# One even state of eight handled like the odd ones in a selective-scan recurrence

## The reference, cut to what matters

```python
delta = softplus(dt @ w_dt)
deltaA = exp(delta[..., None] * A)                       # decay, one per state n of 16
deltaBu = delta[..., None] * B[:, :, None, :] * u[..., None]   # input, "drive"
def step(h, ab):
    a, bu = ab
    h = a * h + bu
    return (h, h)
...                                                      # scan over the 128 steps of a sequence
y = einsum('bldn,bln->bld', hs, C) + u * D               # states weighed by C, summed over n
return y * silu(res) @ w_out
```

## Time and profile before

| what | value |
|---|---|
| median of three runs | 2059.17 us |
| the profiled execution's own time | 2061.6 us |
| its span | 2059.8 us |
| PE busy | 1955.6 us (95%) |
| VectorE busy | 1422.5 us (69%) |
| GpSimd busy | 1208.6 us (59%) |
| ScalarE busy | 929.9 us (45%) |
| first scan starts, last close starts | 1352.1 us, 1744.40 us |
| scans on VectorE | 128 of 1224 ns and 128 of 1196 ns |

### The profile page before, as it was taken

One profiled execution on the slowest core, in us unless ns is written; L12 is line 12 of the kernel. 1 busy time (PEld: TensorE's weight loads), 2 busy tenths in 40 slices (PEclk: granted clock), 3 DMA queues, 4 the chain that ended last, 5 costly groups with the idle time before them and its releaser, 6 DMA issues. The chain is left out here.

```text
span 2059.8 us, 41932 instructions
## 1 busy us (share of the span) xinstructions
PE 1955.6 (95%) x15620; PEld 1425.1 (69%) x15620; DVE 1422.5 (69%) x1479; ACT 929.9 (45%) x1332; POOL 1208.6 (59%) x862
## 2 busy tenths in 40 slices
PE   6989999999999999999998879989999999999998
PEld 5867777777777777777775557755555655758886
DVE  4126766676666666766766753489999999538775
ACT  4124444444444444444444544276677664533330
POOL 4126666666666666666656740069998997424210
PEclk9999999999999999999998889999999999999999
DMA  5545565555555555555544311040031002111201
GB/s 188 161 133 175 156 181 161 174 163 176 166 164 175 162 177 155 180 153 176 160 145 144 101 52 39 3 123 1 1 89 35 1 1 73 48 61 62 76 27 41
DMA packets 180570, 229.58 MB, mean 111 GB/s; under 512 B 21488, under 2 KB 111920, under 8 KB 174224
## 3 DMA queue, kind: packets, MB, share of 16 engines
q1 hardware_dynamic: 180368, 226.82, 35.7%
HBM read 153.18 MB, written 73.56 MB: 110 GB/s over the span
## 5 line engine op out<-in xcount | busy, mean ns | idle before, releaser
L504 POOL TENSOR_TENSOR a_half<-a_pt 128x1024 f32<-128x1024 f32 x128 | 307.1, 2399 | 345.8 <-ACT a_pt L571 336.3
L571 ACT ACTIVATE a_pt<-a_shift 128x2048 f32<-128x2048 f32 x128 | 245.1, 1915 | 475.4 <-PE a_o L887 371.7
L685 DVE TENSOR_TENSOR a_shift<-a_s,a_neg_rows 128x2048 f32<-128x2048 f32 x113 | 259.0, 2292 | 170.2 <-ACT a_neg_rows L588 170.2
L672 DVE TENSOR_REDUCE a_top<-a_s 128x128 f32<-128x2048 f32 x113 | 258.7, 2290 | 47.3 <-PE a_s L840 47.3
L1274 POOL TENSOR_TENSOR s_even_drive<-s_du,l_rows 128x512 f32<-128x512 f32 x128 | 162.9, 1273 | 61.6 <-DMA s_c_row<-bc_scratch 59.9
L799 PE MATMUL a_pj<-l_x_hi,l_w_hi 128*128 128x512 f32 x448 | 198.3, 443 | 0.0
L495 POOL TENSOR_TENSOR l_x_lo<-a_raw,l_x_hi 128x512 fp32r<-128x512 f32 x120 | 153.1, 1276 | 72.5 <-ACT l_x_hi L558 72.5
L799 PE MATMUL a_pj<-l_w_hi,l_x_hi 128*128 128x512 f32 x448 | 185.2, 413 | 0.0
L1282 POOL TENSOR_TENSOR s_odd_seen<-s_odd_state,s_c_row 128x512 f32<-128x512 f32 x128 | 162.5, 1270 | 34.9 <-DVE s_odd_state L1413 15.1
L1474 PEld LDWEIGHTS s_ps<-s_diag,s_du_t 128*128 128x128 f32 x1024 | 135.8, 194 | 62.0 <-issue 62.0
L801 PE MATMUL a_pj<-l_x_lo,l_w_hi 128*128 128x512 f32 x448 | 176.9, 395 | 0.1
(11 more groups left out here) (270 smaller groups left out, 4066.7 us busy)
## 6 DMA issues: line engine op xcount, KB each, us to landing
kv_scratch<-a_k_new SPq DMA_DIRECT2D x128, 256.0 KB, 2.5
kv_scratch<-a_v_new SPq DMA_DIRECT2D x128, 256.0 KB, 3.6
a_stack<-kv_scratch SPq DMA_DIRECT2D x512, 64.0 KB, 2.3
a_v<-kv_scratch SPq DMA_DIRECT2D x32, 1024.0 KB, 6.0
a_raw<-in_ctx SPq DMA_DIRECT2D x120, 256.0 KB, 3.3
a_q_stack<-q_scratch SPq DMA_DIRECT2D x128, 64.0 KB, 2.0
s_c_row<-bc_scratch SPq DMA_DIRECT2D x32, 256.0 KB, 5.7
e_ew_raw<-in_ew SPq DMA_DIRECT2D x8, 1024.0 KB, 4.8
```

The lines of the kernel that those rows point to most:

```text
L504: nc.gpsimd.tensor_tensor(half[:], w[:, 0:2], w[:, 2:4], ALU.add).then_inc(halved, 1)
L571: nc.scalar.activation(pt_head(g, p), shift[:].rearrange("p (i n) -> p i n", n=BANK), ACT.Exp).then_inc(exped, 1)
L672: dve.tensor_reduce(top[:], s_ps[:].rearrange("p i n -> p (i n)").rearrange("p (k q) -> p q k", q=L), AX.X, ALU.max).then_inc(blocked, 1)
L685: dve.tensor_tensor(shift[:].rearrange("p (k q) -> p k q", q=L), s_ps[:].rearrange("p i n -> p (i n)").rearrange("p (k q) -> p k q", q=L), ...
```

## The change

The even state of pair 6 (LATE = 6, one of the eight pairs) is made on the way of the odd states, in every tile:

- its input is made by PE, with a diagonal of its own (`late_diag`) that ScalarE makes. PE issues it directly ahead of drive_odd of the same pair, in step k = 5. Both kinds share the two places of `odd_drive`, which are now counted by `turned`, 9 per tile; the inputs of the other even states are counted by `evens`, 7 per tile;
- its decay goes to a buffer of its own in SBUF (`late_decay`), and its state into row block 6 of `rows`, which no longer holds a row of B;
- VectorE scans it (`scan_late`), and has no weigh_even for this pair;
- GpSimd weighs it in place (`weigh_late`), ahead of weigh_odd(6), and has no drive_even for it. drive_even still runs two even states ahead, so pair 7's is issued at k = 4 and the next tile's first at k = 5;
- PE adds it from there, in the place where add_even(6) was;
- SyncE loads one row of B less in each group, and loads block 6 of w_out once the last tile's pair 6 has been added.

```diff
+        late_diag, late_decay = st.sb("late_diag", [P, BG, L]), st.sb("late_decay", [P, BANK])
+        LATE = 6
+        late_state = rows[:, LATE, :]
+        made = ([*range(EARLY, LATE), PAIRS, *range(LATE, PAIRS)], [*range(PAIRS), PAIRS])
+        evens = lambda t, k: (PAIRS - 1) * t + k - (k > LATE)
+        turned = lambda t, k: (PAIRS + 1) * t + k + (k > LATE)
+        turned_to = lambda q: turned(q // PAIRS, q % PAIRS) + 1 + (q % PAIRS == LATE)
 # SyncE, end of the scan
             for k in range(PAIRS):
-                sp.wait_ge(even_driven, PAIRS * (TILES - 1) + k + 1)
+                if k == LATE:
+                    sp.wait_ge(summed, even_sum_no(PAIRS * (TILES - 1) + k))
+                else:
+                    sp.wait_ge(even_driven, evens_to(PAIRS * (TILES - 1) + k))
                 sp.dma_start(rows[:, k, :], w_out[:, k, :]).then_inc(w_out_in, 16)
 # GpSimd
+            def weigh_late(t, k, q):
+                rows_there(t, 2 * k)
+                pool.wait_ge(odd_scanned, turned(t, k) + 1)
+                nc.gpsimd.tensor_tensor(late_state, late_state, c_row[:, 2 * k, :], ALU.mult).then_inc(odd_weighed, 1)
             for t, k, q in steps:
+                if k == LATE:
+                    weigh_late(t, k, q)
                 weigh_odd(t, k, q)
...
-                if q + 2 < len(steps):
-                    drive_even(*steps[q + 2])
+                if k != LATE and evens(t, k) + 2 < len(driven):
+                    drive_even(*driven[evens(t, k) + 2])
 # ScalarE
+                if k == LATE and t >= 1:
+                    act.wait_ge(odd_scanned, turned(t - 1, LATE) + 1)
+                if k != LATE and evens(t, k) >= 2:
+                    act.wait_ge(even_scanned, evens(t, k) - 1)
...
-                if 2 <= q - PAIRS * (DT - 1) < 2 + PAIRS:
-                    make_diagonal(q - PAIRS * (DT - 1) - 2, 1)
+                if 2 <= q - PAIRS * (DT - 1) < 2 + len(made[1]):
+                    make_diagonal(made[1][q - PAIRS * (DT - 1) - 2], 1)
 # VectorE
+            dve.memset(by_batch(late_decay[:])[:, :, 0:1], 0.0).then_inc(zeroed, 1)
+            def scan_late(t, k, q):
+                n = turned(t, k)
+                dve.wait_ge(even_decayed, q + 1)
+                dve.wait_ge(odd_driven, n + 1)
+                if t >= 1:
+                    dve.wait_ge(summed, even_sum_no(q - PAIRS))
+                dve.tensor_tensor_scan(late_state, late_decay[:], odd_drive[:, n % 2, :], 0.0,
+                                       ALU.mult, ALU.add).then_inc(odd_scanned, 1)
             for t, k, q in steps:
-                scan_even(t, k, q)
+                if k == LATE:
+                    scan_late(t, k, q)
+                else:
+                    scan_even(t, k, q)
                 scan_odd(t, k, q)
-                weigh_even(t, k, q)
+                if k != LATE:
+                    weigh_even(t, k, q)
 # PE
-            def drive_odd(t, k, q):
+            def drive(t, n, k):
                 pe.wait_ge(du_t_out, t + 1)
-                if q >= 2:
-                    pe.wait_ge(odd_scanned, q - 1)
+                if n >= 2:
+                    pe.wait_ge(odd_scanned, n - 1)
...
                 for b in range(BG):
-                    mm = pe.matmul(odd_drive[:, q % 2, b * L:(b + 1) * L], du_t[:, t % 2, b], diag[:, k, b],
-                                   start=True, stop=True)
+                    mm = pe.matmul(odd_drive[:, n % 2, b * L:(b + 1) * L], du_t[:, t % 2, b],
+                                   late_diag[:, b] if k == PAIRS else diag[:, k, b], start=True, stop=True)
+            def drive_odd(t, k, q):
+                if k == LATE:
+                    drive(t, turned(t, k), PAIRS)
+                drive(t, turned_to(q) - 1, k)
 # add_even
+                if k == LATE:
+                    pe.wait_ge(odd_weighed, turned(t, k) + 1)
+                else:
+                    pe.wait_ge(even_weighed, evens(t, k) + 1)
```

More of the change, by code:

```diff
@@ L1213, in mixer_scan @@
         row_in = st.sems(*[f"row_in{n}" for n in range(N // 4)])
-        ROWS = 16 * 6
+        ROWS = lambda n: 16 * (5 if n // 4 == LATE // 2 else 6)
         block = ctx.enter_context(nc.Block())
@@ L1226, in mixer_scan @@
         EARLY = 2
[L1228 removed]
+        LATE = 6
+        late_state = rows[:, LATE, :]
+        made = ([*range(EARLY, LATE), PAIRS, *range(LATE, PAIRS)], [*range(PAIRS), PAIRS])
+        diag_no = lambda t, k: BG * (made[0].index(k) + 1 if t < DT else len(made[0]) + made[1].index(k) + 1)
+        evens = lambda t, k: (PAIRS - 1) * t + k - (k > LATE)
+        evens_to = lambda q: evens(q // PAIRS, q % PAIRS) + (q % PAIRS != LATE)
+        turned = lambda t, k: (PAIRS + 1) * t + k + (k > LATE)
+        turned_to = lambda q: turned(q // PAIRS, q % PAIRS) + 1 + (q % PAIRS == LATE)
         even_sum_no = lambda q: max(1, 2 * q)
@@ L1239, in _ @@
                     if g >= 1:
-                        sp.wait_ge(odd_weighed if n % 2 else even_weighed, PAIRS * (DT * g - 1) + n // 2 + 1)
-                    if n % 2 == 0:
+                        q = PAIRS * (DT * g - 1) + n // 2
+                        if n % 2 or n == 2 * LATE:
+                            sp.wait_ge(odd_weighed, turned_to(q))
+                        else:
+                            sp.wait_ge(even_weighed, evens_to(q))
+                    if n % 2 == 0 and n != 2 * LATE:
                         sp.dma_start(b_row[:, n // 2, :], bc_scratch[n, cols].partition_broadcast(P))\
@@ L1283, in weigh_odd @@
                   .then_inc(odd_weighed, 1)
-            for t, k, q in steps[:2]:
-                drive_even(t, k, q)
+            driven = [step for step in steps if step[1] != LATE]
+            for step in driven[:2]:
+                drive_even(*step)
             for t, k, q in steps:
+                if k == LATE:
+                    weigh_late(t, k, q)
                 weigh_odd(t, k, q)
@@ L1353, in _ @@
                     empty_du(0)
-                if t == 0 and k + EARLY < PAIRS:
-                    make_diagonal(k + EARLY, 0)
+                if q < len(made[0]):
+                    make_diagonal(made[0][q], 0)
                 if k == 1 and 1 <= t < TILES - 1:
@@ L1400, in scan_even @@
             def scan_even(t, k, q):
+                n = evens(t, k)
                 dve.wait_ge(even_decayed, q + 1)
-                dve.wait_ge(even_driven, q + 1)
-                if q >= 2:
[L1404 to L1413, removed]
+                dve.wait_ge(even_driven, n + 1)
@@ L1414, in scan_odd @@
+            def scan_odd(t, k, q):
+                n = turned_to(q) - 1
+                dve.wait_ge(odd_decayed, q + 1)
+                dve.wait_ge(odd_driven, n + 1)
+                if q >= 2:
+                    dve.wait_ge(odd_weighed, turned_to(q - 2))
+                dve.tensor_tensor_scan(odd_state[:, q % 2], odd_decay[:, q % 3], odd_drive[:, n % 2, :], 0.0,
                                        ALU.mult, ALU.add).then_inc(odd_scanned, 1)
             def weigh_even(t, k, q):
+                n = evens(t, k)
```

49 lines of the change are left out of this document (27 added, 22 removed).

## The result

The changed kernel takes 2071.1 us (median of 7 runs, 2067.26 to 2074.42) against 2059.17 (7 runs, 2055.07 to 2063.49). The ratio is 1.0057, 95% interval 1.0041 to 1.0073: slower by 8.4 to 15.0 us. Forecast were 2069.4 us, +10.2, in a range of 2063 to 2074.

A forecast was written before the change was run, and what follows sets the result against it. VectorE was taken to bound each tile, with PE level at scan_odd(7). 13 tiles of 0.85 us, less 0.3 and 0.6, gave +10.2 us on the 2059.17 median: 2069.4 us, range 2063 to 2074.

The forecast's parts named there:

- What bounds the kernel: Scan stage: VectorE bounds the 24.09 us tile to within 0.2 us; PE meets it at scan_odd(7), at most 0.11 to spare.
- The drive's price: PE's added drive ahead of drive_odd(6) moves scan_odd(7) by 0.85 us per tile (0.78 to 0.98), in 13 tiles 11.05.
- VectorE's saving: Dropping weigh_even(6) saves VectorE about 0.60 us per tile, eaten by a 1.45 us wait before scan_odd(7).
- The sign in the profile: VectorE waits before scan_odd 1.3 to 1.6 us once a tile, about 14 tiles, some 20 us, released by PE's drives.
- GpSimd 0: GpSimd's late weighing, in place of drive_even(6), costs nothing: it ends 1.2 us before PE asks for it.
- The switch 0: At the group switch VectorE waits for ScalarE, which takes in the delay: tile 7 costs 0, not 0.85.
- Tile 14: Without make_delta, PE's drive has 0.94 us to spare before scan_odd(7): between -0.60 and +0.05, taken as -0.3 us.
- Tile 15: Last tile, without make_delta or turn_du: VectorE's whole saving comes through, -0.6 us.
- w_out and the set-up 0: The w_out load waiting for pair 6's sum is hidden by some 2.5 us; the set-up memset costs 0, at most 0.1.
- Rival 1: PE takes the drive into idle time and each tile gives 0.60 us: -9.6 us, 2049.6 us; chance 0.10.
- Rival 2: Half the drive's price is absorbed; a tile gives -0.2 to +0.4 us, -3 to +5 in all, about 2060; chance 0.09.
- Rival 3: GpSimd's late weighing ahead of weigh_odd(6) binds too: 0.85 + 0.6 us a tile, about +18 us, 2077; chance 0.08.

The follow-up runs named there:

- e3: Kernel before the change, weigh_even of pair 6 done on 8 of 512 columns (VectorE's saving alone): 2057.99 us, ratio 0.9997.
- e1: Kernel before the change, drive_odd of pair 6 issued twice (PE's added work alone): 2070.97 us, ratio 1.0067.
- e7: Changed kernel, GpSimd's weigh_odd of pair 5 done twice, ahead of the late weighing: 2069.61 us, ratio 1.0047 to the kernel before.
- e6: Changed kernel with only one of the four products of the late drive: 2065.99 us, ratio 1.0032.
- e2: Kernel before the change, drive_odd of pair 3 issued twice, ahead of PE's critical stretch: 2058.26 us, ratio 0.9997.
- e5: Changed kernel with LATE = 2, the second group's late diagonal made third instead of last: 2060.27 us, ratio 0.9998 to the kernel before.
- e8: Kernel before the change, weigh_even(6) on 8 columns and make_delta on 128 of 512 columns from tile 2 on: 2052.34 us, ratio 0.9961.
- e4: Changed kernel with pair 2 as the late one (LATE = 2 instead of 6): 2066.72 us, ratio 1.0035.

## Why the prediction was right

*What bounds the kernel.* PE and VectorE meet at scan_odd(7) with 0.11 us or less to spare. Right, and the spare was nearer to 0: with PE late, the scan starts 1.14 us after the drive (1522.00 to 1523.14), before it was 1.16. e3 shows PE level with VectorE there. Of the 0.2 us by which the forecast's 23.9 misses the tile, 0.18 is a wait that it didn't read: scan_even(5) starts 0.76 and not 0.58 us after weigh_even(4), behind GpSimd's drive_even(5). It is there in the changed kernel as well (1514.70 to 1515.46), so it moves nothing here.

*The drive's price.* Taken 0.85 (bounds 0.78 to 0.98), measured 0.89 in PE's stretch and 24.95 - 24.09 = 0.86 in the tile. Ten of the thirteen tiles show 0.83 to 0.86 one by one; tiles 0 to 2, where the start of the stage still shows, paid 0.50, 0.78 and 0.54, the last because the kernel before loses some 0.3 us of its own there. That is 10.3 us for the thirteen, where 11.05 were forecast.

*VectorE's saving.* 0.60 less work, and a wait of 1.45 in its place: from start to start the wait is 1523.14 - (1520.64 + 1.13) = 1.37 us. The missing 0.08 is the scan of the late state, which starts 0.68 and not 0.58 after weigh_even(5): the late drive ends at 1518.30, and it comes 0.1 us late, the "at most 0.1 us" of the forecast. Hidden, since the longer wait follows.

*The sign in the profile.* Forecast a wait in about 14 tiles, some 20 us in all, "released by PE's drives". It is 18.2 us (16.9 and 1.3), 14 times, and the release is PE's (by the timelines, and by e1); but the column says ScalarE. A reader who had gone by the label would have called the prediction wrong. The sign "PE near 98% of the stage" did not come: PE stayed at 97.14 of 100, since its idle time of 0.7 us a tile stayed and the tile grew along with the work.

*GpSimd 0.* Cover forecast 1.2 us, found 1.28; with 1.35 us more on GpSimd, e7 overdraws it by 0.12 at PE's add.

*The switch 0.* Right, +0.01: make_delta ends at 1544.07 + 1.12 = 1545.19 and ScalarE takes it at 1545.57 without waiting; VectorE's wait for ScalarE behind it shrinks from 2.28 us to 1.53. *Tile 14* -0.3: -0.32. *Tile 15* -0.6: only -0.13 up to the last close, the term that was furthest off for its size. Without turn_du and make_delta PE is not late there, so the forecast gave VectorE its whole 0.6, as e3 does (-0.52). But the late drive stands behind PE's adds of pair 4, which wait for VectorE themselves, and from there PE runs without a wait up to drive_odd(7), so nothing hides what it is late: the late scan starts 0.29 us after VectorE is there (1743.28), scan_odd(7) 0.12 (1746.78), both from start to start. With a quarter of the late drive (e6) the last tile takes 15.21 instead of 15.56, close to the 15.17 of e3. The errors, -0.8 in the thirteen tiles and +0.5 here, nearly cancel: +9.84 against +10.2. That the sum came so close is in part luck.

*w_out and the set-up 0.* Nothing shows behind the last close: 315.4 us before and after.

Rival 1 (PE takes it in) falls by e1, and comes true only where PE has idle time, in e2. The Trainium skill (Perfetto Trace Analysis, section Identifying the Most-Contended Engine) judges PE's headroom by MFU (the arithmetic done as a share of the peak) and by the share of time in weight loads. By that share PE had room, 59.2 us of 100 before and 60.75 after. e1 added PE work alone at the critical place and lost all of it, so there the measurement decides against that reading; in e2 the same work was free, so the room existed, and the share does not say where. Rival 2 (half is absorbed) falls by the interval. Rival 3 falls by the 1.28 us of cover, which e7 had to use up before GpSimd's order cost anything.

What stays open: the medians differ by 11.9 us, the stage by 9.84. The interval of the ratio holds both, and no run here says that the rest is more than spread between executions.

## What to carry to other kernels

When two engines meet at one point of a loop, moving work from the fuller to the emptier one pays only if the emptier has its idle time between its last wait and that point; find that stretch in the timeline, add up starts there, and see whether the same work fits ahead of its last wait instead. Duplicating or shortening one instruction on either side, at the place and elsewhere, tells in a few runs which side holds what. And after moving, look for the next limit before pricing the gain: here two PSUM places at pair 6, and at pair 2 the order of the diagonals and a second meeting point.

## What the runs showed of the hardware

- A releaser in the profile can be wrong by the whole cause: 16.9 us in 13 waits stood against a decay that had ended 4.75 us before (1518.39 to 1523.14). The same label came in e1 (0.81) and e3 (0.44), where nothing of ScalarE's was touched.
- PE is a little slower behind a wait. From drive_odd(6) to make_delta it takes 0.98 us when PE runs on (1518.14 to 1519.12), and 1.06 behind the wait in e6 (1489.25 to 1490.31). That 0.08 is why e6 gave back 0.17 and not 0.25.
- PE ran at 99.56 us busy of 100, at a granted clock of 1.00 (2.4 GHz), in e2 and e5: 0.89 us of matmuls a tile at no cost, where 97.14 before the change looked full. Even then its weight load waited 0.3 us a tile.
- A short wait of PE can cost clock behind it, and need not. In e3 and e8 PE waited 2.32 and 2.45 us at the switch of groups and then ran at a granted clock of 0.57 from 1550 to 1554, close to the lower level (1.2 GHz); the kernel before waited 2.32 us there and stayed at 1.00. The same happened behind 4.94 us in e4 and 2.80 us in tile 0 of e5.
